# A two-block graph attention kernel on one core: edge counts from packed one-hots, one exponential per softmax, and a reordered opening

## Time and profile before

| quantity | value |
|---|---|
| median of three runs | 373.2 us (372.81 to 374.55) |
| the profiled execution | 373.22 us, of which the span from first to last instruction is 371.1 us |
| PE busy | 355.4 us (96%) |
| POOL, DVE, ACT busy | 247.6, 219.4, 213.7 us |
| mean granted TensorE clock | 0.998 of full speed |

### The profile page before, as it was taken

One profiled execution on the slowest core, in us unless ns is written; L12 is line 12 of the kernel. 1 busy time (PEld: TensorE's weight loads), 2 busy tenths in 40 slices (PEclk: granted clock), 3 DMA queues, 4 the chain that ended last, 5 costly groups with the idle time before them and its releaser, 6 DMA issues.

```text
span 371.1 us, 6198 instructions
## 1 busy us (share of the span) xinstructions
PE 355.4 (96%) x2104; PEld 304.1 (82%) x2104; DVE 219.4 (59%) x570; ACT 213.7 (58%) x373; POOL 247.6 (67%) x170
## 2 busy tenths in 40 slices
PE   7899979999999999999999999998988999999994
PEld 4788868888988988898898898897666788888883
DVE  3996766428328345543741923736776788763875
ACT  4996466756755664673765665565352667244601
POOL 2789619595866947849668595692268976397911
PEclk9999999999999999999999999999999999999999
DMA  7979936637637536754663752755073256436002
GB/s 250 320 244 262 389 128 197 224 95 250 178 96 257 184 134 180 241 172 126 215 239 98 251 174 91 241 188 204 0 219 134 90 165 193 165 94 242 8 0 85
DMA packets 24544, 65.15 MB, mean 176 GB/s; under 512 B 1952, under 2 KB 3024, under 8 KB 24528
## 3 DMA queue, kind: packets, MB, share of 16 engines
q1 hardware_dynamic: 20720, 55.19, 44.7%
q10 hardware_dynamic: 3808, 9.76, 8.8%
HBM read 64.15 MB, written 0.79 MB: 175 GB/s over the span
## 4 chain that ended last, share of the span: by engine, by line
PE 71%; ACT 7%; DVE 6%; issue 6%; POOL 5%; DMA 4%; SPq 0%; POOLq 0%; DVEq 0%; ACTq 0%
PE ps L918 52%; PE ps L1202 7%; PE ps L1003 6%; DMA raw<-in_L_gnn_W 4%; POOL ring_lo L364 3%; ACT ring_hi L351 2%; PE ps L982 1%; PE ps L1268 1%; PE ps L1036 1%; ACT rows_hc L689 1%; POOL ring_lo L380 1%; ACT z L689 1%; PE ps L968 1%; ACT am L689 1%; POOL x_sb L619 1%
## 5 line engine op out<-in xcount | busy, mean ns | idle before, releaser
L364 POOL TENSOR_TENSOR ring_lo<-raw,ring_hi 128x768 fp32r<-128x768 f32 x94 | 170.7, 1851 | 75.1 <-ACT ring_hi L351 75.0
L351 ACT ACTIVATE ring_hi<-raw 128x768 fp32r<-128x768 f32 x96 | 77.5, 851 | 35.2 <-PE ps L918 28.6
L380 POOL TENSOR_TENSOR ring_lo<-raw,ring_hi 128x512 fp32r<-128x512 f32 (+1 forms) x40 | 59.7, 1521 | 24.0 <-ACT ring_hi L373 23.9
L1402 DVE CUSTOM_DVE_ANT_0 e<-ps,att 128x768 f32<-128x768 f32 (+1 forms) x54 | 40.0, 796 | 51.3 <-PE ps L918 48.7
L918 PE MATMUL ps<-ring_hi,zT_hi 128*128 128x512 f32 (+1 forms) x256 | 69.4, 346 | 0.9 <-DVE zT_lo L1558 0.6
L918 PE MATMUL ps<-ring_lo,zT_hi 128*128 128x512 f32 (+1 forms) x256 | 67.4, 338 | 0.0
L918 PE MATMUL ps<-ring_hi,zT_lo 128*128 128x512 f32 (+1 forms) x256 | 67.2, 338 | 0.0
L918 PE MATMUL ps<-ring_hi,xT_hi 128*128 128x512 f32 x192 | 51.3, 343 | 2.3 <-POOL ring_lo L364 1.0
L918 PE MATMUL ps<-ring_lo,xT_hi 128*128 128x512 f32 x192 | 50.3, 339 | 0.0
L918 PE MATMUL ps<-ring_hi,xT_lo 128*128 128x512 f32 x192 | 50.2, 338 | 0.0
L918 PEld LDWEIGHTS ps<-ring_hi,zT_lo 128*128 128x128 f32 x256 | 43.2, 188 | 5.6
(11 more groups left out here) (163 smaller groups left out, 562.2 us busy)
## 6 DMA issues: line engine op xcount, KB each, us to landing
raw<-in_L_gnn_W SPq DMA_DIRECT2D x54, 768.0 KB, 4.4
raw<-in_L_gnn_Wr SPq DMA_DIRECT2D x8, 768.0 KB, 4.3
att<-in_L_gnn_a_src ACTq DMA_DIRECT2D x10, 384.0 KB, 4.6
att<-in_L_gnn_a_dst ACTq DMA_DIRECT2D x10, 384.0 KB, 5.4
raw<-in_L_gnn_W SPq DMA_DIRECT2D x4, 384.0 KB, 6.1
x_sb<-in_x SPq DMA_DIRECT2D x3, 256.0 KB, 5.7
rows_hc<-in_L_gnn_b SPq DMA_DIRECT2D x1, 512.0 KB, 6.3
rows_hc<-in_L_gnn_g SPq DMA_DIRECT2D x1, 512.0 KB, 7.2
```

Of the source, the lines that this page charges most:

```text
L351: eng.activation(slot_hi(c), raw_chunk(c), ACT.Copy).then_inc(hi_done, 1)
L364: eng.tensor_tensor(slot_lo(c), raw_chunk(c), slot_hi(c).bitcast(F32), ALU.subtract)\
L380: eng.tensor_tensor(ring_lo[:, q["ring_at"]:q["ring_at"] + w], raw[:, q["raw_group"], q["raw_at"]:q["raw_at"] + w], ring_hi[:, q["ring_at" ...
L1402: dve.tensor_tensor_reduce(junk[:, at:at + w], of[:, (k - first_head(a)) * w:(k - first_head(a) + 1) * w], att[:, half_at * row + k * w:ha ...
```

## The change

- **Counts.** The one-hot of an edge group has 128 columns, for the target modulo 128, and its entry is a weight: -1 for a target below 128, 4096 for one above (twice that in the groups whose steps DVE makes). The ramp becomes a step with 257 columns, `sign(n - src + 0.5)` on ACT (ACT function Sign) or plus or minus 0.5 on DVE. One product per edge group, so 32 in all, and none for the self-loops. ACT copies 257 sums; DVE takes one first difference, rounds to a multiple of 4096 by adding and subtracting a large constant, subtracts, adds the self-loops from the identity in two 128-wide instructions, then makes `far`. ACT, not DVE, copies `counts`.
- **Softmax.** The target's score is now scaled by -0.8 (a softmax does not change when `a_d` is taken off every entry of its row): ACT makes `0.2 s - 0.8 a_d` (`leaks`, one Identity per tile), DVE takes the maximum with `s` (`leaky_scores`), then minus that plus `far` with a running minimum (`tile_tops`), and ACT takes one exponential per tile. The four small instructions and the maximum of the exponentials go.
- **Opening.** DVE instead of POOL makes the `lo` halves of chunks 2 and 3. The edges are loaded by SP's queue behind the first `x` part; `b1` is loaded after the first split on ACT's. `scores(0)` moves ahead of the counts. 12 of the one-hots read the bf16 `iota` in SBUF, 20 the f32 copy in PSUM. Chunk 2's product takes its last pass after the wait for `xT_lo`.
- **Head 0.** DVE has three instead of four dot products of head 1 between `pT_lo` and head 0's ELU. PE starts W2's chunks 0 and 1 of head 0 with the second node tile when `zT_hi` is there. ACT used to copy the sums, split W2 chunks 0 to 2, take the exponentials and split chunk 3; it now splits chunks 0 and 1, copies the sums, copies `counts`, takes the exponentials and splits chunks 2 and 3.

```diff
-            for c in (0, 1, 2):
+            leaks(0)
             att_for(1)
-            act.wait_ge(counted, NT)
-            act.activation(ramp_sum, ps[:, COUNT_AT[0]:COUNT_AT[0] + NT * N], ACT.Copy).then_inc(ramps_copied, 1)
+            for c in (0, 1):
                 split_hi(act, 2, c)
+            act.wait_ge(counted, 1)
+            act.activation(step_sums, ps[:, STEPS_AT:STEPS_AT + 1 + N], ACT.Copy).then_inc(sums_copied, 1)
+            act.wait_ge(far_done, 1)
+            act.activation(counts[:, :, :].rearrange("p i n -> p (i n)"), ps[:, COUNT_AT:COUNT_AT + NT * N],
+                           ACT.Copy).then_inc(counts_done, 1)
             exps(0, (1, 0))
...
             for c in range(CH):
                 if c == 2:
+                    scores(0)
                     pe.wait_ge(b1_ready, 2)
-                    count_edges(0, COUNT_HALF)
-                    count_loops()
-                    count_edges(COUNT_HALF, ET)
-                if c == 3:
-                    scores(0)
+                    count_edges()
                 project_chunk(1, 1, c)
...
+            def leaks(a):
+                act.wait_ge(scores_bc, a + 1)
+                for i in range(NT):
+                    act.wait_ge(a_dst_done, before(a) + heads_of(a) * (i + 1))
+                    for k in range(heads_of(a)):
+                        at = s_at(a, k)
+                        act.activation(e1[:, first_head(a) + k, i, :], ps[:, at:at + N], ACT.Identity,
+                                       bias=a_d[:, pair(a, k, i)], scale=SLOPE).then_inc(leak_done, 1)
...
             def hots(first, end):
                 for t in range(first, end):
-                    dve.tensor_scalar(hot(t, 1), iota_ps, edges_f[:, 1, t:t + 1], None, ALU.is_equal)\
+                    of = iota[:, 1:1 + P] if t < HOTS_FROM_SBUF else iota_ps[:, 1:1 + P]
+                    dve.tensor_scalar(hot(t), of, row_of[:, t:t + 1], weight_of[:, t:t + 1], ALU.is_equal, ALU.mult)\
                        .then_inc(hot_done, 1)
...
             def softmax(h):
-                masked_scores(h)
-                projected_lo(h)
+                leaky_scores(h)
+                dve.wait_ge(leaky_done, 2 * h + 2)
+                projected_lo(h, 0)
+                for i in (1, 0):
+                    tile_tops(h, i)
+                projected_lo(h, 1)
                 normalised(h)
                 weights_lo(h)
```

More of the change, by code:

```diff
@@ L188, in build_gnn, with hot, step @@
         per_home = ET // len(hot_homes)
[L190 to L202, removed]
+        def hot(t):
+            at = (t % per_home) * 2 * N
+            return hot_homes[t // per_home][:, at:at + P]
+        def step(t):
+            at = (t % per_home) * 2 * N + P
+            return hot_homes[t // per_home][:, at:at + 1 + N]
+        iota_i = hs[:, 0:1 + N].bitcast(I32)
+        step_sums = hs[:, 2 * N:3 * N + 1]
+        packed = hs[:, 4 * N:5 * N]
         ps = ctx.enter_context(nc.psum_tensor("ps", [P, 8 * BANK], F32))
@@ L680, in _, with steps @@
             act.activation(rstd[:, 0:1], half[:, :], ACT.Exp)
[L681 to L686, removed]
+            def steps(first, end):
                 for t in range(first, end):
-                    bias = edges_f[:, 0, t:t + 1] if t < ET else self_f[:, t - ET:t - ET + 1]
-                    act.activation(ramp(t), iota[:, :], ACT.Relu, bias=bias).then_inc(ramp_act_done, 1)
+                    act.activation(step(t), iota[:, :], ACT.Sign, bias=src_bias[:, t:t + 1]).then_inc(step_act_done, 1)
             def input_hi(b):
@@ L737, in _ @@
             y = [z[:, i * D:(i + 1) * D] for i in range(NT)]
-            def exps(a, order):
[L741 to L747, removed]
+            def leaks(a):
[6 more added lines that the diff above has]
+                                       bias=a_d[:, pair(a, k, i)], scale=SLOPE).then_inc(leak_done, 1)
+            def exps(a, order):
+                for n, i in enumerate(order):
+                    act.wait_ge(masked, before(a) + heads_of(a) * (n + 1))
+                    for k in range(heads_of(a)):
+                        at = masked_at(a, k, i)
+                        act.activation(at, at, ACT.Exp, bias=top[:, pair(a, k, i)], scale=-1.0).then_inc(e_done, 1)
             def weights_hi(a):
@@ L850, in _ @@
             chunks_hi(0, 2)
-            act.wait_ge(a_dst_done, before(A_CONV2) + 2)
+            leaks(A_CONV2)
             projected_tile_hi(A_CONV2, 1)
@@ L866, in _ @@
             chunks_hi(14, 15)
+            leaks(A_GAT1A)
             exps(A_GAT1A, (0, 1))
@@ L895, in _ @@
             chunks_hi(36, 39)
+            leaks(A_GAT2)
             features_hi(A_GAT2, tiles=(1,))
@@ L1084, in _, with count_edges @@
                 project_chunk(FIRST_PHASE, 0, c, at=ACC)
[L1086 to L1088 removed]
+            def count_edges():
+                for t in range(ET):
                     pe.wait_ge(hot_done, t + 1)
[L1090 to L1098 removed]
@@ L1127, in _, with first_accumulate, rest_of_head @@
             aggregate_T(0)
+            def first_accumulate(c, i, passes=ALL):
+                return product(ACC, i, node_tile(zT_hi, c, i), node_tile(zT_lo, c, i), slot_hi(c), slot_lo(c),
+                               False, False, passes=passes)
+            pe.wait_ge(z_hi_done, 1)
+            for c in (0, 1):
+                chunk(2, c)
+                first_accumulate(c, 1, passes=FIRST_TWO)
             pe.wait_ge(z_lo_done, 1)
             clear_acc(0)
-            def rest_of_head(h, scores_at=1):
-                for c in range(CH):
+            for c in (0, 1):
+                first_accumulate(c, 1, passes=LAST_ONE)
+                first_accumulate(c, 0).then_inc(chunk_used, 1)
+            def rest_of_head(h, scores_at=1, first=0):
+                for c in range(first, CH):
                     if c == scores_at:
@@ new lines, in leaky_scores, with tile_tops @@
+                dve.wait_ge(leak_done, before(a) + NT * n)
+                for i in range(NT):
+                    for k in range(n):
+                        at = s_at(a, k)
+                        dve.tensor_tensor(masked_at(a, k, i), ps[:, at:at + N], e1[:, first_head(a) + k, i, :], ALU.max)\
+                           .then_inc(leaky_done, 1)
+            def tile_tops(a, i):
+                n = heads_of(a)
+                for k in range(n):
+                    if isinstance(a, int):
+                        dve.wait_ge(leaky_done, before(a) + n * i + k + 1)
+                    at = masked_at(a, k, i)
+                    dve.tensor_tensor_reduce(at, at, far[:, i, :], -1.0, 3.0e38, ALU.add, ALU.min, top[:, pair(a, k, i)])\
+                       .then_inc(masked, 1)
```

273 lines of the change are left out of this document (126 added, 147 removed).

## The result

| | before | after |
|---|---|---|
| median | 373.0 us (372.23 to 374.55, 6 runs) | 375.95 us (375.22 to 376.3, 6 runs) |
| profiled execution, span | 373.22, 371.1 | 375.9, 374.1 |
| mean granted TensorE clock | 0.998 | 0.987 |

The ratio is 1.0079, with an interval of 1.0063 to 1.0096: the changed kernel is 0.8% slower, where the prediction said 369.9 (368.3 to 373.3) and gave "slower by over 0.5%" a chance of 0.06. Single executions of some kernels lay far above all others (389.8 to 1985.6 us); the ratios leave them out.

A forecast was written before the change was run, and what follows sets the result against it. It took PE, busy for 96% of the span, as the bound, with DVE's chain only 0.4 us shorter. Terms -2.7 - 0.8 + 0.6 - 0.6 + 0.2 = -3.3 took the median of 373.2 to 369.9 us, range 368.3 to 373.3.

The forecast's parts named there:

- When PE can start it: Opening: halved one-hots cost 0.20 to 0.40 us; first dot product at 24.5, a_s at 26.3, counts at 26.0.
- signs of being wrong: The forecast is wrong if DVE's queue, not ACT's, orders the opening, or if head 1's lost 0.6 us stays.
- Rival 3: Opening: each one-hot from SBUF waits for a POOL subtraction (1.85 us), dot products at 28.6, time 373.5; chance 0.13.
- PE's counting: Counts on PE: 32 products of 257 columns at 0.109 us each take 3.5 us, 3.6 less than before.
- ACT's queue does not follow: Opening on ACT: splits stand ahead of the copy of the sums, ending at 33.0; PE 3.7 us earlier, the copy 1.1.
- Head 0's ELU: Between aggregate_T(0) and scores(1): three dot products ahead instead of four gain 0.75 us; W2's early start takes nothing off.
- The softmaxes: Head 1 loses 0.6 us, which comes back; heads 2 to 7 fit by 0.55; block 0's last layer gains or loses little.
- Moved loads: Opening: b1, issued 2.5 us later, can hold PE up by 1 us, which the room ahead of the counts covers.
- rival 1: Opening: ACT's queue is not the bound, so PE's 3.9 us and the ELU's 0.8 come through, 368.7; chance 0.14.
- rival 2: On ACT: a second table load; chance 0.08.
- rival 4: Heads 2 to 7, at weights(h): softmax outgrows PE's cover of 0.55 us; 375.6 if 1.5 us late; chance 0.10.

The follow-up runs named there:

- e1: The changed kernel with four instead of 12 one-hots read from SBUF (4 to 11 from the f32 copy in PSUM): 369.61 us, ratio 0.9898.
- e12: e9 with eight instead of four one-hots read from SBUF (4 to 7 changed): 375.43 us, ratio 1.0059.
- e8: The changed kernel with 20 instead of 12 one-hots read from SBUF, a single execution: 378.46 us.
- e2: The changed kernel with 26 products of zeros on PE ahead of scores(0), to keep it busy: 374.56 us, ratio 1.0029.
- e4: e1 with ACT's copy of the sums ahead of the two splits of W2's chunks 0 and 1: 370.28 us, ratio 0.9907.
- e10: e9 with the fourth dot product put back ahead of head 0's ELU on DVE: 369.36 us, ratio 0.9889.
- e11: e9 without PE's early start of W2's chunks 0 and 1 with zT_hi: 368.43 us, ratio 0.9862.
- e6: e1 with head 0's h_hi, leaks and the copy of the sums ahead of the splits of chunks 4 and 5 on ACT: 368.63 us, ratio 0.9858.
- e9: e6 with b1's load issued first on ACT, as in the kernel before: 368.14 us, ratio 0.9852.
- e3: The kernel before with one-hots 4 to 11 (256 columns) read from the bf16 iota in SBUF: 373.53 us, ratio 0.9994.
- e7: The changed kernel with scores(0) put back behind chunk 2, its 12 one-hots still from SBUF: 375.28 us, ratio 1.0034.

## Why the prediction was wrong

**The step that failed** is "When PE can start it", and in it the price of a one-hot. It took 0.20 to 0.40 for all 32, from a row in which DVE reads PSUM, and put the first dot product at 24.5. Twelve of them read SBUF. Four of these took 1.83 each because POOL was subtracting, so the dot product came at 28.87, 4.4 later than forecast. With one-hots 4 to 11 from PSUM it comes at 23.77 (e1). That DVE's queue and not ACT's orders the opening is one of the signs of being wrong that the prediction named.

**Rival 3 had the course of events, and a chance of 0.13.** Its estimate, one one-hot from SBUF for each POOL subtraction under way (1.85 each), gave: last of them at 22, dot products at 28.6, `a_s` at 30.4; the last one from SBUF ended at 22.6, the dot products began at 28.87, and PE had `a_s` at 30.76. The row that bore it out, 1.63 beside POOL against 0.68 without, was read and given little weight. It is a single pair and shows no price per subtraction; the changed kernel, e12 and e8 do, with one one-hot for each subtraction of 1.82 us. From PSUM they took 0.32 each whether or not POOL worked (e1). The runs show that the source (its place, or the type that came with it) and the overlap matter; what makes the one engine wait for the other they do not show.

**Its time was 2.4 too low (373.5 against 375.9).** The term left out is the clock. The rival let the counts end at 34, at the full rate; they ended at 37.4. PE had been idle for 5.75 us, and the products ran at a granted clock of 0.50. Against e1, `weights(0)` stands 6.7 later: 5.0 for the late start, 0.3 for the slow transposes, 2.3 for the slow counts, less 0.7 that PE waited for DVE there in e1 and 0.2 in the chunks. e2 measures the clock alone: 2.5 between `scores(0)` and `weights(0)`, 1.4 in the medians.

**The other steps**, seen in e1, where the one-hots no longer hide them:

| step | predicted | e1 |
|---|---|---|
| counts on PE, start and length | 26.0, 3.5 | 25.98, 3.9 |
| copy of the sums ends | 33.0 | 32.90 |
| `far` ends | 36.1 | 36.06 |
| division ends | 39.2 | 39.16 |
| `weights(0)` | 39.2 (2.7 gained) | 39.22 (2.7) |
| `weights(0)` to `scores(1)` | 0.8 less | 0.64 less |
| `scores(1)` to `weights(1)` | 0.6 more | 0.59 more (7.41 against 6.82) |
| regained by `weights(2)` | 0.6 | 0.94 |
| `weights(2)` to the end | 0.2 more | 0.26 more |
| median | 369.9 | 369.61 |

- *PE's counting*: 3.9, not 3.5, at the full clock (0.12 each, not 0.109). In e1 DVE's chain covers the difference.
- *When PE can start it*, with the one-hots from PSUM: 26.0 is right in part by luck. `a_s` is there at 25.6, not 26.3, and PE, a microsecond ahead otherwise, has lost 0.99 waiting for `b1`.
- *ACT's queue does not follow*: right in place and time, incomplete in reason. It named the splits ahead of the copy; e4 shows that `h_hi`, and DVE's `h_lo` behind it, was as late.
- *Head 0's ELU*: right in both parts, by e10 (0.76 against 0.75) and e11 (0 against 0).
- *The softmaxes*: right. In head 2 of the kernel after the division ends at 95.12 and PE needs it at 95.62, a cover of 0.5 where 0.55 was counted.
- *Moved loads*: "covered" was wrong. In the profiled execution of the kernel after `b1` is in time; in e1's PE waits 0.99 for it, in e6's 0.66. DVE's one-hots stand behind it, so in e9, without that wait, the first dot product and `weights(0)` come 0.55 and 0.58 earlier than in e6, and the medians differ by 0.5.
- *Rivals 1, 2 and 4*: none happened. Every run has one table load, of 1.28 us, so no run shows the second load behind rival 2's chance of 0.08. The gain that rival 1 names was to be had by reordering ACT (e6), not by itself.
- *Chances*: 0.06 for slower came from rival 4 alone. Rival 3 stood under "same" with its 373.5, because its price held nothing for what an idle PE costs afterwards.

## What to carry to other kernels

Price a VectorE instruction by where its operands are and by what GpSimd does in that very stretch, not by its columns: a 0.23 us instruction cost 1.83, and only where the two overlapped; from an f32 copy in PSUM it cost 0.32 with and without overlap. Look at the gaps, since the same line is cheap a microsecond later (0.2 each in e3). Where a wait of several microseconds is moved to TensorE, add the slow clock after it (here a granted 0.50 for some 6 us of products after 5.75 us idle, 2.5 us up to `weights(0)` by e2); reordering TensorE does not remove such a wait if the chain on the other engine is late (e7). When two paths are equally long, shorten both: of the one alone, here the copy's, nothing came (e4, e6).

## What the runs showed of the hardware

- A bf16 one-hot of 128 columns from SBUF took VectorE 0.23 us with GpSimd idle, and one GpSimd subtraction (1.82 us) each with GpSimd at work: 7.41 and 6.76 us for four of them in two kernels. From an f32 copy in PSUM it took 0.32 in both cases. GpSimd's own instructions were not longer for it: four in 7.28 us, 7.26 in e1.
- After TensorE had been idle for 5.75 us the granted clock was 0.50 for some 6 us of products; after 6.10 us idle in e12 for 4.4, and after 4.87 us idle in another place (e7) for 4.7. With products of zeros in the idle stretch (e2) it stayed at 1.00.
- ACT's Sign and Exp ran with a single table load of 1.28 us in every run, at 0.74 in the changed kernel.
